# LoRA-B rows of the gate/up matrices gathered in two runs of feature tiles, later gathers placed behind gate/up steps

## What is computed

```python
x = x + conv(x * mask, K) * mask                      # K: 64 channels x 1024 taps
gate = x @ W_gate.T + ((x @ A_gate[r].T) @ B_gate[r].T) * 0.5
up   = x @ W_up.T   + ((x @ A_up[r].T)   @ B_up[r].T)   * 0.5
act  = silu(gate) * up                                # 2752 features
x = x + act @ W_down.T + ((act @ A_down[r].T) @ B_down[r].T) * 0.5
```

## Time and profile before

| | us |
|---|---|
| median of 3 runs | 1744.29 (1742.24 to 1745.56) |
| the profiled execution | 1744.96 |
| its span, first to last instruction | 1743.3 |
| PE busy | 1634.4 (94%) |
| DVE busy | 921.3 (53%) |
| ACT busy | 565.8 (32%) |
| POOL, time in issuing its DMAs and little else | 109.0 (6%) |
| DMA, whole kernel | 278.42 MB, 160 GB/s on average |

### The profile page before, as it was taken

How to read it: one execution, slowest core, us unless ns; L and a number is a source line. 1 busy time by engine, 2 the same in 40 slices (tenths; PEclk the granted TensorE clock), 3 DMA queues, 4 the chain that set the end, 5 groups by cost and what they waited for, 6 DMA issues and landing times.

```text
span 1743.3 us, 20961 instructions
## 1 busy us (share of the span) xinstructions
PE 1634.4 (94%) x8224; PEld 1399.2 (80%) x8224; DVE 921.3 (53%) x1182; ACT 565.8 (32%) x678; POOL 109.0 (6%) x169
## 2 busy tenths in 40 slices
PE   1988969999999999699999999998999999999999
PEld 1988857888888888578888888886888888888887
DVE  6444466665666655676655666566325325424422
ACT  2211234333333333353333333334224224324321
POOL 4300063410000000000000000000000000000000
PEclk9999979999999999799999999998999999999999
DMA  8998677743333333433333333326547547646652
GB/s 300 359 352 327 213 240 214 224 142 97 97 97 102 107 107 109 134 95 97 107 107 105 108 103 101 97 73 209 171 130 229 168 139 219 178 135 217 180 139 61
DMA packets 157637, 278.42 MB, mean 160 GB/s; under 512 B 56323, under 2 KB 73539, under 8 KB 156995
## 3 DMA queue, kind: packets, MB, share of 16 engines
q1 hardware_dynamic: 104034, 234.19, 42.1%
q0 software_dynamic: 13440, 25.86, 4.8%
q10 hardware_dynamic: 40064, 17.04, 3.5%
HBM read 237.26 MB, written 65.31 MB: 174 GB/s over the span
## 4 chain that ended last, share of the span: by engine, by line
PE 87%; DMA 6%; DVE 4%; issue 2%; ACT 1%; SPq 0%; DVEq 0%; ACTq 0%
PE ps L769 80%; PE ps L754 6%; DMA tt<-k_pad 2%; DMA k_pad<-ksb 1%; DMA x_keep<-xt 1%; DMA raw<-a_gu_sel 1%; DMA xraw<-x_keep 1%; ACT whi L963 1%; DVE xlo L1485 1%; DVE wlo L1485 1%; DMA draw<-act_keep 0%; DVE xraw L1485 0%; DMA raw<-wgu 0%; ACT b12hi L963 0%; DVE xres L1679 0%
## 5 line engine op out<-in xcount | busy, mean ns | idle before, releaser
L769 PE MATMUL ps<-xhi,whi 128*128 128x512 f32 (+1 forms) x1080 | 421.5, 390 | 27.0 <-ACT cc L963 10.9
L769 PE MATMUL ps<-xlo,whi 128*128 128x512 f32 (+1 forms) x1080 | 420.4, 389 | 0.0
L769 PE MATMUL ps<-xhi,wlo 128*128 128x512 f32 (+1 forms) x1080 | 419.1, 388 | 0.0
L963 ACT ACTIVATE whi<-raw 128x1024 fp32r<-128x1024 f32 (+3 forms) x202 | 198.0, 981 | 581.5 <-PE ps L769 545.2
L1485 DVE TENSOR_TENSOR wlo<-raw,whi 128x1024 fp32r<-128x1024 f32 (+1 forms) x190 | 219.2, 1155 | 307.2 <-ACT whi L963 306.9
L769 PE MATMUL ps<-dhi,whi 128*128 128x512 f32 (+2 forms) x760 | 288.0, 379 | 3.7 <-DVE xres L1679 3.7
L769 PE MATMUL ps<-dlo,whi 128*128 128x512 f32 (+2 forms) x760 | 286.6, 377 | 0.0
L769 PE MATMUL ps<-dhi,wlo 128*128 128x512 f32 (+2 forms) x760 | 286.4, 377 | 0.0
L769 PEld LDWEIGHTS ps<-xhi,whi 128*128 128x128 f32 x1080 | 207.3, 192 | 66.4 <-issue 11.2
L769 PEld LDWEIGHTS ps<-xhi,wlo 128*128 128x128 f32 x1080 | 206.6, 191 | 41.5
L769 PEld LDWEIGHTS ps<-xlo,whi 128*128 128x128 f32 x1080 | 207.3, 192 | 37.4
(11 more groups left out here) (167 smaller groups left out, 1670.4 us busy)
## 6 DMA issues: line engine op xcount, KB each, us to landing
raw<-wgu SPq DMA_DIRECT2D x84, 512.0 KB, 6.6
tt<-k_pad SPq DMA_DIRECT2D x64, 512.0 KB, 9.7
raw<-wd SPq DMA_DIRECT2D x64, 512.0 KB, 3.8
loraw<-bgu_sel SPq DMA_DIRECT2D x84, 256.0 KB, 4.4
act_keep<-up SPq DMA_DIRECT2D x42, 512.0 KB, 3.1
draw<-act_keep SPq DMA_DIRECT2D x84, 256.0 KB, 7.1
bgu_sel<-bgu POOLq DMA_DIRECT2D x32, 336.0 KB, 7.1
raw<-wd SPq DMA_DIRECT2D x32, 320.0 KB, 3.0
```

The lines of the kernel that those rows point to most:

```text
L769: return nc.tensor.matmul(out, w, x, start=start, stop=stop, skip_group_check=True)
L963: return nc.scalar.activation(out, in_, ACT.Copy)
```

## The change

The B rows of token groups 0 and 1 are gathered in two runs: tiles 0 to 5 (96 KB a sequence in place of 336 KB) with the rest of `gather_gu` from the start, tiles 6 to 20 (240 KB a sequence) by 16 DMAs of their own, `gather_rest`, once the first product of step 0 is done. The gathers for token groups 2 and 3 now wait for the first product of steps 2 and 4, and those for down for that of steps 6, 8, 10 and 12, in place of the end of the convolution alone. SP gets one more wait, ahead of the load of tile 6's rows; the counts of its two later waits grow by the 16 added DMAs.

```diff
+        FIRST = 6
+        REST_SEL = 16 * 16
@@ SP, the loop over steps n
+                if n + 1 == FIRST:
+                    sp.wait_ge(s_gat, 2 * GU_SEL + REST_SEL)
                 if (n + 1) % FT:
                     wait_lo("lora", n)
                     load_lora(n + 1)
                 if n == FT - 2:
-                    sp.wait_ge(s_gat, 4 * GU_SEL)
+                    sp.wait_ge(s_gat, 4 * GU_SEL + REST_SEL)
@@ SP, ahead of down
-            sp.wait_ge(s_gat, 4 * GU_SEL + 4 * DN_SEL)
+            sp.wait_ge(s_gat, 4 * GU_SEL + REST_SEL + 4 * DN_SEL)
@@ POOL
-            def gather_gu(j):
+            def gather_gu(j, tiles):
                 for b8 in range(8):
 ...
-                    pool.dma_start(bgs_d[j, :, r0:r0 + RANK, :, g, :], bgu_d[r]).then_inc(s_gat, 16)
+                    pool.dma_start(bgs_d[j, 0:tiles, r0:r0 + RANK, :, g, :], bgu_d[r, 0:tiles]).then_inc(s_gat, 16)
+
+            def gather_rest(j):
+                for b8 in range(8):
+                    r, g, b, r0 = adapter(j, b8), b8 // BG, b8 % BG, (b8 % BG) * RANK
+                    pool.dma_start(bgs_d[j, FIRST:FT, r0:r0 + RANK, :, g, :], bgu_d[r, FIRST:FT]).then_inc(s_gat, 16)
@@
-            gather_gu(0)
+            gather_gu(0, FIRST)
             pool.wait_ge(s_gat, GU_SEL)
-            gather_gu(1)
-            pool.wait_ge(s_cev, H)
+            gather_gu(1, FIRST)
+            pool.wait_ge(s_p, prod(0, "P1"))
+            pool.wait_ge(s_gat, 2 * GU_SEL)
+            gather_rest(0)
+            gather_rest(1)
             for j in range(2, SW):
-                pool.wait_ge(s_gat, GU_SEL * j)
-                gather_gu(j)
+                pool.wait_ge(s_p, prod(2 * j - 2, "P1"))
+                pool.wait_ge(s_gat, GU_SEL * j + REST_SEL)
+                gather_gu(j, FT)
             for j in range(SW):
-                pool.wait_ge(s_gat, GU_SEL * SW + DN_SEL * j)
+                pool.wait_ge(s_p, prod(2 * j + 6, "P1"))
+                pool.wait_ge(s_gat, GU_SEL * SW + REST_SEL + DN_SEL * j)
                 gather_down(j)
```

## The result

The median fell from 1744.92 us (1742.24 to 1745.95, 4 runs) to 1728.33 us (1727.99 to 1730.85, 4 runs): 16.6 us less, a ratio of 0.991 with a 95% interval of 0.9893 to 0.9928. The forecast was 1735.3 us with a range from 1729.5 to 1742.5. The sign and most of the places were right; the gain was nearly twice the sum of 9.0 us, and 1.2 us beyond the range.

A forecast was written before the change was run, and what follows sets the result against it. Up to 276 us the chain jumps between engines, with PE short of work where POOL's gathers lie; then PE's long run bounds. Terms 2.0 + 4.0 + 3.0 + 0 = 9.0 us gave 1735.3 us, range 1729.5 to 1742.5.

The forecast's parts named there:

- term 1: First taps' write to DRAM, less gather 0 beside it: saves 2.5 us, less 0.5 at first Toeplitz tile; net 2.0.
- term 4: Gathers at their new places under the steps, the rest on the last features' stores: costed at 0, -1 to +2 us.
- term 2: Convolution seams: stall ahead of channel 16 goes, tile for channel 24 comes sooner; 4.0 us, bounds 2.0 and 6.0.
- term 3: Behind the convolution: last quarter of x stored 2.5 us faster, first weight block 0.5; 3.0 us, from 0 to 3.4.
- second seam: Convolution, channel 31's end to channel 40's tile: same 6 MB without any gather, 24.5 us, the measure for channel 24's seam.
- More is gained: Rival, 12%: every byte taken out of 36 to 108 us comes back, store and taps at lower bounds; 14 us or more.
- The early gathers don't get shorter: Rival, 14%: landing hardly depends on size, so gather 0 ends nearly as now; only 3 us gained, 1741.3.
- The gathers spoil the steps: Rival, 6%: SP's loads land late beside gathers in the steps, PE waits for weights; 1753 us.
- nothing to measure: Rival, 8%: the seams close at other limits and all terms fall to their lower bounds; 1743 to 1745 us.

The follow-up runs named there:

- rest at the convolution's end: Changed kernel, but the rest of groups 0 and 1 starts at the convolution's end, not behind step 0's first product: 1731.79 us, ratio 0.9933.
- early half alone: Changed kernel, but gathers 2 and 3 start at the convolution's end, the rest of 0 and 1, then down's, behind step 0's first product: 1734.73 us, ratio 0.9939.
- late half alone: Kernel before, with only the change's POOL waits ahead of gathers 2 and 3 and of down's: 1739.38 us, ratio 0.9966.
- whole gathers behind the taps: Kernel before, with POOL starting gather 0, whole, only when the first taps have landed: 1748.31 us, ratio 1.0025.
- three tiles: Changed kernel with the first run at 3 tiles in place of 6: 1729.75 us, ratio 0.992.

## Why the prediction was right or wrong

**Right: what bounds, and that the steps hide the gathers.** POOL's gathers were the cause at the places named, the stall of 2.03 us ahead of channel 16 is gone, and the long PE runs are unchanged to 0.2 us. SP met no wait at `load_lora(6)`, and weight blocks that landed in 8 to 10 us beside a whole gather were not waited for. Of the 8.0 us that the profiled pair gained beyond the sum of 9.0, 4.65 are term 1's and 2.0 term 4's; 3.0 are not shown to be the change's (2.2 in the convolution, 0.8 behind the start of PE's long run); 1.1 go off again at the first channels, and terms 2 and 3 came out some 0.5 us short.

**Wrong in size: term 1, the first taps.** I put 2.0 us (-1.2 to 4.2), of which 2.5 in the write; up to PE's start it was 6.65 us. The step that failed is the bound: I took 3.0 us, another store's landing, as the least that the write could need, and chose the middle to 6.4. With no gather left beside it, it lands in 1.56 to 1.74 us in seven kernels. The 3.0 us of the earlier trace rows were no floor: that store was issued among SP's first loads. The Trainium skill, DMA: Bandwidth & Descriptors, section Latency and other measured facts, says that access to the memory behind DRAM tensors takes 0.2 us on average and 2 us at high load, and is the main part of a DMA's fixed cost. The runs agree in direction, 1.6 us alone against 6.4 to 11.4 in traffic, but the step is larger than that. Gather 1's bytes cost the first tile nothing (4.06 us against 4.21); the half us put down for that was not needed. Another 1.0 us came ahead of the write and was in no term (below). The two first channels gave back 1.1 us (7.52 us against 6.38); why is open, since with the same gathers up to there they took 6.64 us in the kernel with the rest at the convolution's end and 7.78 in the early half alone.

**Right in size, but it is not a term of its own: term 2.** From channel 8 to channel 24 I put 4.0 us, and 3.75 came. The kernel's second seam served as the measure, and that it gave so near a number is partly luck: the seam took 24.5 us in the trace used, 24.2 in the early half alone, and 22.5 to 22.8 in the seven other kernels without a gather in it. By the late half's trace, with the gathers of before up to there, the same reckoning would have put over 5 us. And I added term 2 to term 1 as if the start were kept whatever happens behind. The whole gathers behind the taps show that it isn't: with a start 7.1 us earlier, channel 24 came 4.8 us later. The two terms are tied: one hangs on what of gather 0 is left at the taps' write, the other on what of both is left when the full stretch begins.

**Not shown to be the change's: 2.2 us from channel 24 to the end of the convolution.** I had put 0. That stretch took 104.9 us before and 102.7 after; in the late half alone, whose gathers are there as before, 101.7, in the early half alone, with those of after, 104.1. It varies by that much between executions with no gather in it. Of the difference 1.7 us lie in the second seam (24.5 against 22.8 us) and 1.05 in the run of channels 40 to 47 (21.30 us at a mean granted clock of 0.87 against 20.25 at 0.92); 0.7 went the other way in that of channels 24 to 31 (20.03 at 0.93 against 20.77 at 0.89). How much of the medians' 16.6 us is of this kind no run shows.

**Right: term 3.** 3.0 us put, 2.7 came (2.1 in the last quarter of x, 0.6 to the set-up's PE run).

**Wrong: term 4, at the stores of the last features.** I put 0 (-1 to +2 us of loss), as gathers would lie on them now too. A gain of 1.9 us came. The step that failed is that a gather issued at that time would load the stores as one in full flow does. ACT waits for these two stores, and they land in 3.0 us (median) in the changed kernel against 4.7. The views of the stores' landing, before and then after, from 245 to 276 us:

```profile
act_keep<-rsg SPq DMA_DIRECT2D x2, 128.0 KB, 4.7
```

```profile
act_keep<-rsg SPq DMA_DIRECT2D x2, 128.0 KB, 3.0
```

The rest's first DMA is issued at 251.56 and the stores at 252.72 and 256.4; q0 moves 0.49 MB until 256, next to nothing from there to 258, and picks up only at 266. Before, q0 moved 1.21 MB in the 8 us from the first store's issue. So the stores cross before POOL is at speed. ACT's wait is 0.63 to 0.68 us in all seven kernels whose gathers 2 and 3 are late, and 2.52 to 3.30 in the three where gathers 2 and 3 follow the convolution's end and others come behind them.

**The rivals.** *More is gained* came true, for the reason it named only in part: not every byte came back (0.4 MB a gather less with three tiles bought nothing), but the taps' write fell below its bound. *The early gathers don't get shorter* fell: gather 0's last packet came at 27.5 us against 34.7, and 16 DMAs more cost nothing. DMAs of 96 and 16 KB landed in 5.7 and 5.3 us where 336 and 16 KB had taken 10.8 and 9.2: landing still depended little on a DMA's own size, but on all that was in flight with it. Reading as a cost per DMA was the trap. The Trainium skill, DMA: Bandwidth & Descriptors, section Anatomy of one DMA, gives 2.0 us fixed for each DMA; what fell is the estimate worked out from it here, which added these up as if the DMAs followed one another. The landings here, 5.3 to 10.8 us, are also above the 2.2 to 2.8 us that it gives for one DMA of these sizes. What does stay per DMA is POOL's issuing, some 20 us for the 24 of gather 0. *The gathers spoil the steps* fell with the long runs, and *nothing to measure* with the interval.

## What to carry to other kernels

Don't add up seams that lie behind one another on the same DMA engines: find the stretch in which they are full, count the bytes that an early transfer still has to move in it (here 2 to 3 us a MB), and look for room ahead of it or behind it rather than for an early start. A small store on the chain, here 32 KB in short runs, costs not what its bytes do but what stands beside it: 1.6 us alone and 6 to 11 us in traffic, so a lower bound for it has to come from an idle machine. A gather that only later tiles need can be cut and put under compute-bound steps; here that cost nothing, with the rest landed by 295 us and its first use at 360.

## What was not expected of the hardware

The taps were issued 1.0 us earlier with the shorter gathers. Part of it is the length-array's load, which lands 0.35 us sooner; that is not the change's, as it lands so in the late half alone too, with the gathers of before (2.81 us against 3.17). The rest is DVE. Some of its short operations take longer when POOL issues a DMA at that moment. The same operation from the groups of instructions of 5 to 26.5 us, before, and of 4 to 27 us with no POOL DMA in it (the whole gathers behind the taps), mean ns of one:

```profile
L1334 DVE TENSOR_SCALAR sm_angk<-sm_ang 128x128 f32<-128x128 f32 x1 | 0.7, 694 | 0.0
...
L1310 DVE TENSOR_SCALAR eki<-sm_ek 128x128 int32<-128x128 f32 x1 | 0.6, 645 | 0.0
```

```profile
L1335 DVE TENSOR_SCALAR sm_angk<-sm_ang 128x128 f32<-128x128 f32 x1 | 0.2, 227 | 0.0
L1311 DVE TENSOR_SCALAR eki<-sm_ek 128x128 int32<-128x128 f32 x1 | 0.2, 226 | 0.0
```

694 and 645 ns against 227 and 226: over 0.4 us each. In the timeline of before the second of them starts while POOL issues a DMA, and ends 0.03 us after that issue does:

```profile
6.41 1.01 POOL L715 DMA_DIRECT2D bgu_sel<-bgu  x1
6.80 0.65 DVE L1310 TENSOR_SCALAR eki<-sm_ek 128x128 int32<-128x128 f32 x1
```

The Trainium skill, SBUF — State Buffer, section SBUF: two separate sides, says that a pair of ports is shared by the two engines as a lock, for DVE instructions of certain kinds, and whichever starts first holds off the other; these rows agree, with DVE the one that waits. In the late half alone, with the same gathers as before, other operations were hit and the taps were issued at 27.12, so the 1.0 us are partly luck. With short gathers they were issued at 26.71 to 26.86 in six kernels, and at 26.42 and 26.50 in the two where POOL starts only behind the taps.
